# Edge lists of a graph attention layer: third quarter's rest shared by eight lanes, and five pieces of work moved to other steps

## The chip, the cores and the metric

One core of one Trainium2 chip. The metric is the device time of one execution in microseconds (us), median of the runs.

## What is computed

One layer of graph attention, then a second graph layer, over 4096 nodes of 128 features and a 4096 x 4096 matrix `adj`:

```python
h = jnp.maximum(_layernorm(x, axis=-1), 0.0)
Wh = h @ W;  e_src = Wh @ a[:d_out];  e_dst = Wh @ a[d_out:]
e = leaky_relu(e_src[:, None] + e_dst[None, :], 0.2)
mask = (adj > 0) | eye(N);  e = where(mask, e, NEG_INF)
x = x + softmax(e, axis=1) @ Wh
h = jnp.maximum(_layernorm(x, axis=-1), 0.0)
weights = where(adj < 1.0, sens(adj), 0.0)      # sens(0) = 0
x = x + weights @ (h @ W1 + B)
```

`adj` holds zeros and ones and is sparse. Where every entry is at least 1 or has a sensitivity of zero, the second layer adds nothing. So the kernel checks every entry (is it 0 or at least 1?), and only if a check, or one of the bounds on list lengths, fails, does it run a general path. These inputs don't take that path.

## The kernel before

**The stream.** `adj` is 64 MB and is read once, in 32 chunks of 2 MB (128 x 4096 fp32) into a ring of six (`adj_ring`), by SyncE's queue. Four quarters (s = 0 to 3) of 1024 rows each have eight chunks: 16 steps of two chunks. Chunks 24 to 31 are the fourth quarter. A slot of the ring is loaded again when its chunk was packed by TensorE and checked by VectorE (13 chunks, line 1129, one pass) or ScalarE (19 chunks, line 947, two passes).

**Packing and scanning.** TensorE turns eight rows' edges and the column number into one word per column (`pack`, L629 and L642). VectorE takes the eight largest words of every segment (`scan`, L1172), and, at the end of a piece of steps, the largest of these (`pick`, L1191): the edges of a lane of eight rows.

**Own and shared slots.** Five pieces (`PIECES`: steps, slots, own, shared, lanes). The first slots of each lane are its own: groups of 8 gathers. What is beyond them (the rest) is merged over 4 or 8 lanes, as many as the last number says (`place` merges on TensorE, L699; `pick_shared` takes the best 32 on VectorE, L1221 to L1249; `place_shared`, L719; `decode_shared` makes the index, L1278, and the masks). A group of shared slots has 32 / lanes gathers: 8 with four lanes, 4 with eight.

**Groups.** In all ten, g = 0 to 9. Piece 1: groups 0, 1 and shared 2; piece 2: 3, 4 and shared 5; piece 3 (third quarter): own group 6, shared group 7; piece 4 (steps 12 to 14): own group 8, its rest being handed to piece 5 (step 15): shared group 9, gathered one by one. For each, GpSimd issues one indirect DMA per slot (L544, 128 rows of the node table each), in the order of the groups. Group g waits until group g - 4 was scattered. Then `weigh` on VectorE (edge weights L1348, L1351; spreading to lanes, L1359, L1365 or L1372) and `scatter` on TensorE (L769) add them to the quarter's sums in PSUM. `add_columns` (L754) and `add_own` (L761) add two further parts; `epilogue` (VectorE, L1453 and L1458) divides and adds to x; a store follows.

**The order.** Each engine runs a loop over the chunks, i = 0 to 31, with what it does at i from tables by hand (`SCAN_AT`, `WEIGH_AT`, `SCATTER_AT`, `EPILOGUE_AT`, `CHECK_LATE` and so on). In VectorE's loop the order at one i is: early checks, `decode`, `decode_shared`, `column` (L1442), `scan`, `pick`, late checks (`CHECK_LATE`), hub, `weigh`, `epilogue`. At the end of its loop VectorE has `weigh(7)`, `scan(15)`, `pick(4)`, `epilogue(2)`, `pick_shared(4)`, `decode_shared(4)`, `weigh(8)` and then group 9 slot by slot, with the fourth quarter's result in three parts (`weigh_last`, L1387 and L1398; `finish_last`, L1468 and L1472).

Of the kernel before, what the change touches and what calls it, by code (L numbers as in the profile page):

```python
# [74 lines left out]
PIECES = [((0, 1, 2, 3), 32, 16, 32, 4), ((4, 5, 6, 7), 24, 16, 16, 4), ((8, 9, 10, 11), 24, 8, 32, 4),  # L75
# [46 lines left out]
CHECK_LATE = {22: 22, 27: 26, 29: 28}  # L122
# [6 lines left out]
QUAD_SCORES_AT, PAIR_SCORES_AT, OCT_SCORES_AT = 2, 4, 5  # L129
# [7 lines left out]
WEIGH_AT = {13: 0, 17: 1, 18: 2, 21: 3, 25: 4, 26: 5, 28: 6}  # L137
SCATTER_AT = {14: 0, 17: 1, 19: 2, 22: 3, 26: 4, 27: 5, 30: 6}
# [3 lines left out]
ADD_COLUMNS_AT = {13: 0, 21: 1, 28: 2}  # L142
EPILOGUE_AT = {20: 0, 28: 1}
OWN_WEIGHTS_AT = {8: 0, 17: 1, 22: 2, CHUNKS: 3}
ADD_OWN_AT = {13: 0, 21: 1, 29: 2}


def gnn_program(nc, x, adj, w0, a0, w1, b1, out):
# [13 lines left out]
    with ctx:  # L162
# [3 lines left out]
        def sem(name):  # L166
# [73 lines left out]
        r_quad = sb("r_quad", [P, 2, KB * 32])  # L240
# [50 lines left out]
        oct_on = shared_on[:, (len(SHARES) - 1) % 2, :, :, :].rearrange("p e k q -> p (e k q)").rearrange(  # L291
            "p (e k c) -> p e k c", k=KB, c=OL)
# [5 lines left out]
        s_by_oct = general_mem[:, NB * 32:NB * 32 + KB * KB * OL]  # L298
# [252 lines left out]
        def _(pe):  # L551
# [121 lines left out]
            def hub_group(m):  # L673
                pe.wait_ge(hub_w_set, m + 1)
                if m == 0:
                    pe.wait_ge(r_quad_set, 5)
# [44 lines left out]
            def quad_scores(pair):  # L721
                if pair:
                    pe.wait_ge(r_quad_set, 1)
                pe.wait_ge(s_by_quad_set, 1)
                pe.wait_ge(shared_set, 7)
                if pair:
                    nc.tensor.matmul(bank[7][:, 0:KB * 32], same_pair, s_by_quad[:, KB * 32:2 * KB * 32], start=True,
                                     stop=True).then_inc(quads_done, 1)
                else:
                    nc.tensor.matmul(bank[7][:, :], same_quad,  # L730
                                     s_by_quad.rearrange("p (h o n) -> p o h n", h=2, o=2)[:, 0, :, :], start=True,
                                     stop=True).then_inc(quads_done, 1)

            def oct_scores():
                pe.wait_ge(r_quad_set, 3)
                pe.wait_ge(s_by_oct_set, 1)
                pe.wait_ge(oct_set, 4)
                nc.tensor.matmul(bank[7][:, :], same_oct, s_by_oct, start=True, stop=True).then_inc(quads_done, 1)
# [78 lines left out]
            for i in range(CHUNKS):  # L817
                pack(i)
                if chunk(i)[0] == 0 and i % 2 == 0:
                    if i == 0:  # L820
                        pe.wait_ge(r_rows_set, 2)
                    turn_hub(i)
                if chunk(i)[1] == 0:
                    turn_columns(i)
                if i == QUAD_SCORES_AT:
                    quad_scores(0)
                if i == PAIR_SCORES_AT:
                    quad_scores(1)
                if i == OCT_SCORES_AT:
                    oct_scores()  # L830
# [18 lines left out]
            scatter(7)  # L849
# [53 lines left out]
        def _(act):  # L903
# [110 lines left out]
            for i in range(CHUNKS):  # L1014
                for s, half in ROW_WEIGHTS_AT.get(i, ()):
                    row_weights(s, half)
                if i == QUAD_SCORES_AT + 1:
                    act.wait_ge(quads_done, 1)
                    nc.scalar.activation(r_quad[:, :, :].rearrange("p s n -> p (s n)"), bank[7][:, :], ACT.Exp,
                                         scale=-(1 - SLOPE)).then_inc(r_quad_set, 1)  # L1020
                if i == PAIR_SCORES_AT + 1:
                    act.wait_ge(quads_done, 2)
                    for h in range(2):
                        part = slice(h * P // 2, (h + 1) * P // 2)
                        nc.scalar.activation(r_pair[part, :].rearrange("p (u n) -> p u n", u=HK),
                                             bank[7][part, 0:KB * 32].rearrange("p (u h n) -> p h u n", u=HK, h=2)[:, h, :, :],
                                             ACT.Exp, scale=-(1 - SLOPE)).then_inc(r_quad_set, 1)
                if i == OCT_SCORES_AT + 2:
                    act.wait_ge(quads_done, 3)
                    for h in range(2):  # L1030
                        part = slice(h * P // 2, (h + 1) * P // 2)
                        nc.scalar.activation(r_oct[part, :].rearrange("p (u n) -> p u n", u=HK),
                                             bank[7][part, :].rearrange("p (u h n) -> p h u n", u=HK, h=2)[:, h, :, :],
                                             ACT.Exp, scale=-(1 - SLOPE)).then_inc(r_quad_set, 1)
# [5 lines left out]
                if i == CHUNKS - 1:  # L1040
                    own_weights(SG - 1)
# [38 lines left out]
        def _(dve):  # L1080
# [127 lines left out]
            def pick_shared(n):  # L1208
# [4 lines left out]
                merge_to = oct_words[:, LEFT:LEFT + w] if n == HANDED + 1 else shared_cand[0:sets, 0:w]  # L1213
# [38 lines left out]
            def decode_shared(n):  # L1252
# [4 lines left out]
                on = oct_on if lanes == OL else shared_on[:, o % 2, 0:w, :, :]  # L1257
# [67 lines left out]
            def edge_weights(g):  # L1325
# [3 lines left out]
                if g == 0:  # L1329
                    dve.wait_ge(r_slots_set, 1)  # L1330
                    dve.wait_ge(r_quad_set, 5)
                if IS_SHARED[g]:
                    o = SHARES.index(n)
                    dve.wait_ge(shared_on_set, o + 1)
                    per = KB * HK
                    r_of = (r_quad[:, s // 2, :] if w == KB else r_pair[:, :]).rearrange("p (e n) -> p e n", n=per)
                    weight = shared_w[:, 0:w, :, :].rearrange("p e k q -> p e (k q)")
                    on = shared_on[:, o % 2, 0:w, :, :].rearrange("p e k q -> p e (k q)")
# [14 lines left out]
            def spread_weights(g):  # L1353
# [10 lines left out]
                elif w == GE:  # L1364
# [4 lines left out]
                        ALU.mult).then_inc(spread_set, 1)  # L1369
                else:  # L1370
# [9 lines left out]
            def weigh_last(e):  # L1380
# [8 lines left out]
                                               oct_on[:, e, :, :].rearrange("p k c -> p (k c)"), ALU.max,  # L1389
# [147 lines left out]
            for n, (col, op, neg) in enumerate(((DD, ALU.max, False), (DD, ALU.min, True),  # L1537
# [8 lines left out]
            quads = (SG - 1) * KB  # L1546
# [9 lines left out]
            nc.vector.tensor_tensor(s_by_oct.rearrange("p (n x) -> p n x", n=KB),  # L1556
                                    whe[:, quads:NB, SS:SS + 1].broadcast_to([P, KB, KB * OL]),
                                    kc_of_m.rearrange("p (o k) c -> p o (k c)", o=1).broadcast_to([P, KB, KB * OL]),
                                    ALU.mult).then_inc(s_by_oct_set, 1)

            for i in range(2, CHUNKS):
# [42 lines left out]
            pick(4)  # L1604
            epilogue(2)
# [107 lines left out]
```

## Time and profile before

| | us |
|---|---|
| median of 3 runs (lowest, highest) | 216.37 (216.04, 217.75) |
| the profiled execution's time | 217.44 |
| its span | 215.6 |
| VectorE busy | 182.0 (84%) |
| ScalarE busy | 189.3 (88%) |
| TensorE busy | 154.3 (72%) |
| GpSimd busy | 132.8 (62%) |
| chain that ended last: DMA, VectorE, TensorE | 36%, 31%, 18% |
| adjacency loads, 32 | 67 MB of 76.8 MB in all |

All instants below are us from the span's start, of the one profiled execution. The chain of work that ended last has the stream of `adj_ring` until 165.4, and from then on pieces of VectorE and TensorE, with GpSimd's gathers between 202.4 and 208.5. Idle time matters only where that chain runs.

### The profile page before, as it was taken

The page shows a single profiled execution, that of the slowest core. Times are in us where ns is not written, and L with a number is a line of the kernel's source. Part 1 is how long each engine was busy: PE and PEld are TensorE (multiplying, and loading weights), DVE is VectorE, ACT ScalarE, POOL GpSimd, SP SyncE. Part 2 cuts the span into 40 slices and gives each one's busy share as a digit, 9 for nine tenths or more (in the row PEclk, how much of TensorE's full clock was granted, in tenths as well). Part 3 has the DMA queues.
Part 4 walks back from the last instruction along what each step waited for, and adds up shares of the span by engine and source line. Part 5 has one row for each costly group of instructions (what it writes and reads, how often), then busy time and mean ns, then how long its engine had stood idle before and what let it go on. Part 6 is the DMA issues. An engine that isn't in the chain of part 4 may idle for free.

```text
span 215.6 us, 3229 instructions
## 1 busy us (share of the span) xinstructions
PE 154.3 (72%) x956; PEld 103.7 (48%) x970; DVE 182.0 (84%) x535; ACT 189.3 (88%) x207; POOL 132.8 (62%) x140
## 2 busy tenths in 40 slices
PE   0186779983794992989929997499392977799472
PEld 0074565440362760549615844186341654668361
DVE  7993999999979999999488796995986499878855
ACT  0699987599899999999999999799999994999960
POOL 3980002295000588888878888888787788667450
PEclk9999999996599698599985999999979799999995
DMA  5999999999999999999999999999999999961303
GB/s 166 355 413 410 410 408 408 409 411 405 418 418 409 409 393 405 391 400 393 402 388 387 394 401 394 404 387 400 394 387 389 386 401 393 406 229 43 115 23 103
DMA packets 22259, 76.81 MB, mean 356 GB/s; under 512 B 2527, under 2 KB 3126, under 8 KB 22240
## 3 DMA queue, kind: packets, MB, share of 16 engines
q1 hardware_dynamic: 18912, 71.31, 84.7%
q0 software_dynamic: 2912, 5.22, 7.0%
q8 instruction: 8, 0.13, 0.2%
q10 hardware_dynamic: 416, 0.07, 0.2%
q14 instruction: 11, 0.09, 0.1%
HBM read 74.06 MB, written 4.23 MB: 363 GB/s over the span
## 4 chain that ended last, share of the span: by engine, by line
DMA 36%; DVE 31%; PE 18%; issue 7%; ACT 5%; SPq 1%; POOL 1%; POOLq 0%; DVEq 0%
DMA adj_ring<-in_adj 35%; DVE summed L1134 10%; PE bank L642 9%; DVE cand L1172 3%; ACT spread L921 3%; DVE hub_w L1415 3%; PE bank L769 2%; DVE x_sb L1458 2%; PE bank L754 2%; PE bank L761 2%; SPq L383 1%; DMA gathered_rows<-node_table,shared_index 1%; DVE stats L1114 1%; PE bank L629 1%; DVE shared_slots L1230 1%
## 5 line engine op out<-in xcount | busy, mean ns | idle before, releaser
L544 POOL DMA_INDIRECT gathered_rows<-node_table,index x48 | 76.0, 1584 | 36.5 <-DVE index L1309 22.5
L952 ACT ACTIVATE trash_a<-adj_ring,below_one 128x4096 fp8e4<-128x4096 f32 x19 | 70.4, 3705 | 5.7 <-DMA adj_ring<-in_adj 5.2
L642 PE MATMUL bank<-adj_ring,pack_w 128*128 128x512 bf16 (+3 forms) x255 | 70.0, 402 | 2.4 <-DMA adj_ring<-in_adj 1.5
L961 ACT ACTIVATE trash_a<-adj_ring 128x4096 fp8e4<-128x4096 f32 x19 | 68.7, 3614 | 0.5
L1134 DVE SCALAR_TENSOR_TENSOR summed<-adj_ring 128x4096 fp8e4<-128x4096 f32 x13 | 58.0, 4458 | 4.3 <-DMA adj_ring<-in_adj 4.2
L642 PEld LDWEIGHTS bank<-adj_ring,pack_w 128*128 128x128 bf16 x262 | 26.1, 104 | 31.5 <-issue 8.8
L544 POOL DMA_INDIRECT gathered_rows<-node_table,shared_index x24 | 33.2, 1382 | 9.6 <-issue 6.7
L1172 DVE MAX8 cand<-bank 128x8 f32<-128x120 f32 (+25 forms) x82 | 23.3, 351 | 3.9 <-PE bank L642 3.9
L769 PE MATMUL bank<-gathered_rows,spread 128*128 128x129 f32 x160 | 20.9, 282 | 3.9 <-DVE spread L1398 2.4
L769 PEld LDWEIGHTS bank<-gathered_rows,spread 128*128 128x128 f32 x160 | 19.4, 194 | 5.1 <-issue 4.8
L629 PE MATMUL bank<-codes,code_w 128*128 128x512 bf16 x25 | 11.2, 448 | 8.5 <-DMA adj_ring<-in_adj 5.6
L678 PE MATMUL bank<-whe,hub_w 128*128 128x129 f32 x64 | 10.4, 316 | 5.1 <-DVE hub_w L1419 5.0
L921 ACT ACTIVATE spread<-x_sb,shift,rstd 128x128 f32<-128x128 f32 x32 | 13.2, 497 | 0.3 <-DVE shift L1126 0.3
L678 PEld LDWEIGHTS bank<-whe,hub_w 128*128 128x128 f32 x64 | 9.1, 219 | 7.0 <-DVE hub_w L1419 6.8
L491 POOL PARTITION_ALL_REDUCE ends_all<-ends x1 | 1.4, 1442 | 17.3 <-DVE ends L1539 17.3
L565 PE MATMUL bank<-ident,spread 128*128 128x128 f32 x32 | 6.3, 327 | 7.8 <-ACT spread L921 7.8
L577 PE MATMUL bank<-w_sb,gathered_rows 128*128 128x130 f32 x64 | 9.8, 300 | 1.4 <-ACT whe L935 1.3
L1442 DVE SCALAR_TENSOR_TENSOR col_w<-r_rows,hub_whe,bank 128x512 f32<-128x512 f32 (+1 forms) x6 | 4.2, 708 | 7.4 <-PE bank L609 7.4
L629 PEld LDWEIGHTS bank<-codes,code_w 128*128 128x128 bf16 x32 | 3.7, 115 | 13.7 <-DMA adj_ring<-in_adj 6.2
L577 PEld LDWEIGHTS bank<-w_sb,gathered_rows 128*128 128x128 f32 x64 | 8.6, 208 | 2.7 <-ACT gathered_rows L927 2.4
L985 ACT ACTIVATE own_w<-ident,w_self 128x128 f32<-128x128 f32 x32 | 9.7, 386 | 0.0
L699 PE MATMUL bank<-slots,own_lane 128*32 128x16 f32 (+1 forms) x24 | 1.4, 188 | 10.5 <-issue 10.5
(190 smaller groups left out, 258.4 us busy)
## 6 DMA issues: line engine op xcount, KB each, us to landing
adj_ring<-in_adj SPq DMA_DIRECT2D x32, 2048.0 KB, 23.6
node_table<-gathered_rows POOLq DMA_DIRECT2D x4, 520.0 KB, 8.3
x_sb<-in_x SPq DMA_DIRECT2D x8, 256.0 KB, 5.9
out<-x_sb SPq DMA_DIRECT2D x3, 512.0 KB, 14.2
gathered_rows<-node_table,index POOLq DMA_INDIRECT x48, 5.9
gathered_rows<-node_table,shared_index POOLq DMA_INDIRECT x24, 5.4
out<-x_sb SPq DMA_DIRECT2D x2, 192.0 KB, 2.1
out<-x_sb SPq DMA_DIRECT2D x1, 128.0 KB, 1.9
```

What stands on the lines that cost most here:

```text
L544: pool.indirect_dma_start(out=rows[:, g % RING_GROUPS * GE + t, :], out_offset=None, in_=table, in_offset=bass.IndirectOffsetOnAxis(ap=row ...
L577: last = nc.tensor.matmul(bank[6 + half][:, b * (D + 2):(b + 1) * (D + 2)], hT[:, nb * P:(nb + 1) * P], w0_sb[:, :], start=(b == 0), stop= ...
L629: nc.tensor.matmul(to[:, :], code_w[:, 2 * c + half, :], codes[:, :], start=True, stop=False, skip_group_check=True)
L642: last = nc.tensor.matmul(to[:, lo:hi], pack_w[:, k, :], ring_hi[:, i % AR, row_at + lo:row_at + hi], start=False, stop=(k == KB - 1), ski ...
L678: last = nc.tensor.matmul(bank[7][:, 0:E1], hub_w[:, m % 2, b, :], whe[:, 4 * HUB_ORDER[m] + b, ONE:ONE + E1], start=(m + b == 0), stop=(m ...
L769: return nc.tensor.matmul(acc_of(SUPER_OF_GROUP[g], t), spread[:, g % 2, at * KB:(at + 1) * KB, :], rows[:, g % RING_GROUPS * GE + turn, G ...
L921: last = nc.scalar.activation(hn_block(b), x_sb[:, b, :], ACT.Identity, bias=shift[:, b:b + 1], scale=rstd[:, b:b + 1])
L952: nc.scalar.activation(trash_a[:, :], ring[:, i % AR, :], ACT.Sign, bias=below_one[:, :], scale=-1.0, accum_out=signs[:, n:n + 1], saturat ...
L961: nc.scalar.activation(trash_a[:, :], ring[:, i % AR, :], ACT.Abs, accum_out=sizes[:, n:n + 1], saturate=False).then_inc(checked_a, 1)
L985: last = nc.scalar.activation(own_w[:, t, :], ident[:, :], ACT.Copy, scale=w_self[:, nb:nb + 1])
L1134: nc.vector.scalar_tensor_tensor(trash_v, ring[:, i % AR, :], 1.0, ring[:, i % AR, :], ALU.is_ge, ALU.not_equal, accum_out=bad_v[:, n:n + ...
L1172: last = nc.vector.max(cand[:, at * 8:(at + 1) * 8], word_bank(step, half)[:, lo:hi])
```

## The change

- Piece 3 merges its rest over eight lanes (`PIECES`, last number 4 to 8). Group 7 then has 4 gathers, not 8; `place(2)` merges eight pieces, not four; `pick_shared(2)` works on 16 x 128 words. Its table of scores is an "oct" one: two of these are made now (`s_by_oct`, `r_oct2`), and the quad and pair scores take one half of a bank each, at one step.
- VectorE checks chunk 26 at step 26 (was 27), chunk 28 at 28 (was 29). In one step the order becomes hub, `epilogue`, `weigh`, late check.
- `weigh(6)` at 27 (was 28), `weigh(7)` at 28 (was behind the loop); `scatter(4)`, `(5)`, `(6)`, `(7)` at 25, 26, 28, 29 (were 26, 27, 30, behind the loop).
- `add_columns(2)`, `add_own(2)` and `epilogue(1)` at 27 (were 28, 29, 28).
- `epilogue(2)` at 31, ahead of `scan(15)` (was behind `pick(4)`).
- `own_weights(3)` on ScalarE at 29, ahead of the check of chunk 29 (was ahead of that of chunk 31).

```diff
-((4, 5, 6, 7), 24, 16, 16, 4), ((8, 9, 10, 11), 24, 8, 32, 4),
+((4, 5, 6, 7), 24, 16, 16, 4), ((8, 9, 10, 11), 24, 8, 32, 8),
-CHECK_LATE = {22: 22, 27: 26, 29: 28}
+CHECK_LATE = {22: 22, 26: 26, 28: 28}
-QUAD_SCORES_AT, PAIR_SCORES_AT, OCT_SCORES_AT = 2, 4, 5
+QUAD_SCORES_AT, OCT_SCORES_AT = 2, (4, 5)
-WEIGH_AT = {13: 0, 17: 1, 18: 2, 21: 3, 25: 4, 26: 5, 28: 6}
-SCATTER_AT = {14: 0, 17: 1, 19: 2, 22: 3, 26: 4, 27: 5, 30: 6}
+WEIGH_AT = {13: 0, 17: 1, 18: 2, 21: 3, 25: 4, 26: 5, 27: 6, 28: 7}
+SCATTER_AT = {14: 0, 17: 1, 19: 2, 22: 3, 25: 4, 26: 5, 28: 6, 29: 7}
-ADD_COLUMNS_AT = {13: 0, 21: 1, 28: 2}
-EPILOGUE_AT = {20: 0, 28: 1}
-OWN_WEIGHTS_AT = {8: 0, 17: 1, 22: 2, CHUNKS: 3}
-ADD_OWN_AT = {13: 0, 21: 1, 29: 2}
+ADD_COLUMNS_AT = {13: 0, 21: 1, 27: 2}
+EPILOGUE_AT = {20: 0, 27: 1, 31: 2}
+OWN_WEIGHTS_AT = {8: 0, 17: 1, 22: 2, 29: 3}
+ADD_OWN_AT = {13: 0, 21: 1, 27: 2}
...
+                elif SET_LANES[PIECE_OF_GROUP[g]] == OL:
+                    for x in range(2):
+                        last = nc.vector.tensor_tensor(
+                            spread[:, g % 2, x * w * KB:(x + 1) * w * KB, :].rearrange("p e (o c) -> p e o c", o=2),
+                            oct_w[:, 0:w, :, :].rearrange("p e k (o c) -> p (e k) o c", o=1).broadcast_to(
+                                [P, w * KB, 2, OL]),
+                            quad_of_e[:, 2 * x:2 * x + 2].rearrange("p (o q c) -> p o q c", o=1, c=1).broadcast_to(
+                                [P, w * KB, 2, OL]), ALU.mult)
+                    last.then_inc(spread_set, 1)
...
             dve.wait_ge(oct_set, 2)
-            nc.vector.tensor_tensor(s_by_oct.rearrange("p (n x) -> p n x", n=KB),
...
+            for n in range(2):
+                blocks = slice((2 + n) * KB, (3 + n) * KB)
+                nc.vector.tensor_tensor(s_by_oct[n].rearrange("p (n x) -> p n x", n=KB),
...
+                for m in HUB_AT.get(i, ()):
+                    hub(m)
+                if i in EPILOGUE_AT:
+                    epilogue(EPILOGUE_AT[i])
+                if i in WEIGH_AT:
+                    weigh(WEIGH_AT[i])
                 if i in CHECK_LATE:
                     check(CHECK_LATE[i])
-                for m in HUB_AT.get(i, ()):
-                    hub(m)
-                if i in WEIGH_AT:
-                    weigh(WEIGH_AT[i])
-                if i in EPILOGUE_AT:
-                    epilogue(EPILOGUE_AT[i])
-            weigh(7)
             scan(STEPS - 1)
             pick(4)
-            epilogue(2)
             pick_shared(4)
```

## Rows read from the trace of the kernel before

**Rows 1.** Page, the span in 40 slices of 5.39 us: busy share of the DMA engines

```profile
DMA  5999999999999999999999999999999999961303
```

**Rows 2.** The 32 adjacency loads: from issue to landing

```profile
DMA to landing us min/median/max: 11.1/23.6/27.2
```

**Rows 3.** VectorE's timeline: start, us, line, operation, idle time before and its releaser

```profile
164.76 0.73 DVE L1372 TENSOR_TENSOR spread<-same,hq_of_e 128x512 f32<-128x512 f32 x1
169.84 0.75 DVE L1442 SCALAR_TENSOR_TENSOR col_w<-r_rows,hub_whe,bank 128x512 f32<-128x512 f32 x1 [4.35 <-PE bank L609]
170.51 4.42 DVE L1134 SCALAR_TENSOR_TENSOR summed<-adj_ring 128x4096 fp8e4<-128x4096 f32 x1
...
176.78 0.20 DVE L1348 TENSOR_TENSOR edge_w<-r_slots,gathered_rows 128x64 f32<-128x64 f32 x1
...
177.28 1.22 DVE L1359 TENSOR_TENSOR spread<-edge_w,lane_of_p 128x1024 f32<-128x1024 f32 x1
...
180.70 4.42 DVE L1134 SCALAR_TENSOR_TENSOR summed<-adj_ring 128x4096 fp8e4<-128x4096 f32 x1
...
188.86 0.17 DVE L1309 SCALAR_TENSOR_TENSOR index<-words_i,empty_i 128x8 int32<-128x8 int32 x1
...
190.98 0.43 DVE L1348 TENSOR_TENSOR same<-r_quad,gathered_rows 128x256 f32<-128x256 f32 x1 [0.41 <-DMA gathered_rows<-node_table,shared_index]
...
194.59 1.43 DVE L1172 MAX8 cand<-bank 128x8 f32<-128x272 f32 x4 [1.47 <-PE bank L642]
...
196.69 2.16 DVE L1458 SCALAR_TENSOR_TENSOR x_sb<-bank,rden,x_sb 128x128 f32<-128x128 f32 x8
...
202.19 0.16 DVE L1278 TENSOR_TENSOR shared_index<-shared_column,shared_empty 128x4 int32<-128x4 int32 x1
```

**Rows 4.** GpSimd's timeline in the same form: gathers of groups 6 to 9

```profile
166.08 1.00 POOL L544 DMA_INDIRECT gathered_rows<-node_table,index  x1 [0.30 <-issue]
...
171.29 4.50 POOL L544 DMA_INDIRECT gathered_rows<-node_table,shared_index  x1 [0.30 <-issue]
...
177.41 1.97 POOL L544 DMA_INDIRECT gathered_rows<-node_table,shared_index  x1 [0.30 <-issue]
...
180.98 5.01 POOL L544 DMA_INDIRECT gathered_rows<-node_table,shared_index  x1 [0.30 <-issue]
...
189.80 1.08 POOL L544 DMA_INDIRECT gathered_rows<-node_table,index  x1 [2.77 <-DVE index L1309]
...
203.13 1.01 POOL L544 DMA_INDIRECT gathered_rows<-node_table,shared_index  x1 [2.60 <-DVE shared_index L1278]
```

**Rows 5.** TensorE's timeline, same form: chunks 26 and 28 packed, place(4)

```profile
165.46 0.39 PE L629 MATMUL bank<-codes,code_w 128*128 128x512 bf16 x1 [4.03 <-DMA adj_ring<-in_adj]
...
167.49 1.91 PE L642 MATMUL bank<-adj_ring,pack_w 128*128 128x512 bf16 x4
...
177.00 0.39 PE L629 MATMUL bank<-codes,code_w 128*128 128x512 bf16 x1 [1.35 <-DMA adj_ring<-in_adj]
177.23 1.07 PE L642 MATMUL bank<-adj_ring,pack_w 128*128 128x512 bf16 x4
...
196.42 0.54 PE L699 MATMUL bank<-slots,own_oct 128*16 128x8 f32 x16
```

**Rows 6.** From issue to landing, gathers of group 7: at 169.99, then at 180.98

```profile
DMA to landing us min/median/max: 5.4/5.4/5.4
...
DMA to landing us min/median/max: 9.9/9.9/9.9
```

**Rows 7.** One stretch: busy us of PE, PEld, DVE, ACT, POOL; granted clock, DMA, GB/s

```profile
166.00:169.40 3.40, 3.40 (x11) 1.23 (x10) 0.00 (x0) 3.37 (x3) 2.71 (x3) 0.51 1.03 392
```

**Rows 8.** Timeline: table of oct scores on VectorE, its exponentials on ScalarE

```profile
34.56 0.68 DVE L1556 TENSOR_TENSOR spread<-whe,bits_i 128x512 f32<-128x512 f32 x1
...
60.47 0.77 ACT L1032 ACTIVATE r_oct<-bank 64x256 f32<-64x256 f32 x2
```

**Rows 9.** ScalarE's timeline: the first pass of its check of chunk 29

```profile
182.26 3.71 ACT L952 ACTIVATE trash_a<-adj_ring,below_one 128x4096 fp8e4<-128x4096 f32 x1 [3.13 <-DMA adj_ring<-in_adj]
```

More of the change, by code:

```diff
@@ L290, in gnn_program @@
         oct_w = shared_mem.rearrange("p (e k c) -> p e k c", k=KB, c=OL)
-        oct_on = shared_on[:, (len(SHARES) - 1) % 2, :, :, :].rearrange("p e k q -> p (e k q)").rearrange(
-            "p (e k c) -> p e k c", k=KB, c=OL)
+        oct_on = [shared_on[:, o % 2, :, :, :].rearrange("p e k q -> p (e k q)").rearrange(
+            "p (e k c) -> p e k c", k=KB, c=OL) for o in range(len(SHARES))]
         s_by_quad = general_mem[:, 0:NB * 32]
@@ L297, in gnn_program @@
         oct_words = placed[0:LANES, 1, :]
-        s_by_oct = general_mem[:, NB * 32:NB * 32 + KB * KB * OL]
+        s_by_oct = [general_mem[:, NB * 32 + n * KB * KB * OL:NB * 32 + (n + 1) * KB * KB * OL] for n in range(2)]
         verdict = cand[:, 0:NBAD]
@@ L719, in place_shared, with quad_scores, oct_scores @@
                 nc.tensor.matmul(to[:, SHARED_COL:SHARED_COL + TURNS[n]], words, turns, start=True, stop=True, skip_group_check=True).then_inc(shared_done, 1)
-            def quad_scores(pair):
-                if pair:
-                    pe.wait_ge(r_quad_set, 1)
+            def quad_scores():
                 pe.wait_ge(s_by_quad_set, 1)
                 pe.wait_ge(shared_set, 7)
[L726 to L736, printed above, removed]
+                nc.tensor.matmul(bank[7][:, 0:KB * 32], same_quad, s_by_quad[:, 0:KB * 32], start=True,
+                                 stop=True, skip_group_check=True)
+                nc.tensor.matmul(bank[7][:, KB * 32:2 * KB * 32], same_pair, s_by_quad[:, KB * 32:2 * KB * 32], start=True,
+                                 stop=True, skip_group_check=True).then_inc(quads_done, 1)
+            def oct_scores(n):
+                pe.wait_ge(r_quad_set, 3 + 2 * n)
+                pe.wait_ge(s_by_oct_set, n + 1)
                 pe.wait_ge(oct_set, 4)
-                nc.tensor.matmul(bank[7][:, :], same_oct, s_by_oct, start=True, stop=True).then_inc(quads_done, 1)
+                nc.tensor.matmul(bank[7][:, :], same_oct, s_by_oct[n], start=True, stop=True).then_inc(quads_done, 1)
             def add_columns(s):
@@ L825, in _ @@
                 if i == QUAD_SCORES_AT:
[L826 to L830, printed above, removed]
+                    quad_scores()
+                if i in OCT_SCORES_AT:
+                    oct_scores(OCT_SCORES_AT.index(i))
                 if i in PLACE_AT:
@@ L848, in _ @@
                     place(PLACE_BEHIND[i])
-            scatter(7)
             place(4)
@@ L1212, in pick_shared @@
                 source = bank[4] if n == 0 else bank[7]
-                merge_to = oct_words[:, LEFT:LEFT + w] if n == HANDED + 1 else shared_cand[0:sets, 0:w]
+                if n == HANDED + 1:
+                    merge_to = oct_words[:, LEFT:LEFT + w]
+                elif w > 64:
+                    merge_to = oct_words[:, 0:w]
+                else:
+                    merge_to = shared_cand[0:sets, 0:w]
                 words = oct_words[:, 0:LEFT + w] if n == HANDED + 1 else merge_to
@@ L1334, in edge_weights @@
                     dve.wait_ge(shared_on_set, o + 1)
[L1335 to L1338, printed above, removed]
+                    if SET_LANES[n] == OL:
+                        per = KB * OL
+                        r_of = r_oct2[:, :].rearrange("p (e n) -> p e n", n=per)
+                        weight = oct_w[:, 0:w, :, :].rearrange("p e k c -> p e (k c)")
+                        on = oct_on[o][:, 0:w, :, :].rearrange("p e k c -> p e (k c)")
+                    else:
+                        per = KB * HK
+                        r_of = (r_quad[:, :] if w == KB else r_pair[:, :]).rearrange("p (e n) -> p e n", n=per)
+                        weight = shared_w[:, 0:w, :, :].rearrange("p e k q -> p e (k q)")
+                        on = shared_on[:, o % 2, 0:w, :, :].rearrange("p e k q -> p e (k q)")
                 else:
@@ L1545, in _ @@
             dve.wait_ge(shared_set, 7)
-            quads = (SG - 1) * KB
+            quads = 2 * KB
             nc.vector.tensor_tensor(s_by_quad.rearrange("p (n x) -> p n x", x=32)[:, 0:quads, :],
```

35 lines of the change are left out of this document (17 added, 18 removed).

## The prediction

> **What bounds the kernel now.** Read the page's slices first [rows 1]: the 16 DMA engines are full from the second slice to the 35th, up to about 189 us. That is the stream of 32 chunks, and its loads wait 11.1 us at the least between issue and landing [rows 2], so a further load is always queued and a small delay of an engine early on does not starve it. The change can only matter in the last fifth. Then read VectorE's timeline there [rows 3]. VectorE waits for chunk 26 (4.35 us idle), checks it at 170.51, checks chunk 28 from 180.70 to 185.12, and from then on nearly everything hangs on it: the third gather list (index, 188.86), the last scan (194.59, after 1.47 us idle for TensorE), the third epilogue (to 198.85), the last picks and the last list (shared_index, 202.19). Then read GpSimd's [rows 4]: gathers follow each other every 1.30 us (1.00 and 0.30 of issue). Group 8 starts 0.94 us after its index (189.80), and its eight fill GpSimd to 200.53 (the idle of 2.60 before the next); group 9, the last four, starts at 203.13, again 0.94 us after its index. From there to the span's end it is 12.5 us, of which the change alters almost nothing. So **the gain is the number of us by which group 9 starts sooner.**
>
> **The work that hangs on the check of chunk 28.** Call the end of that check E; now E = 185.12. Group 8's first gather starts at E + 4.7. Group 9's starts at E + 18.0.
>
> **The third epilogue goes ahead of the last scan.** It is 2.16 us of updates, and some 0.2 of reciprocals ahead of them. Now it stands between pick(4) and pick_shared(4). It ends at 198.85, while what pick_shared(4) needs, the merge of place(4) on TensorE, is ready at 196.96 [rows 5]; with about 0.1 us for the hand-over this link shortens by 1.7 us. Scan to index(4) takes 7.6 us now (194.59 to 202.19) and would take 5.9. Part of the epilogue moves into the 1.47 us of idle before the scan. weigh(7) (2.14 us, from 190.98 to the 193.12 at which that idle begins) is moved ahead of the check too. So VectorE's chain from E is: the stretch to index(3), 3.7 us; the rest of its decoding and pick_shared(3), to E + 5.45 (190.57 now); epilogue E + 7.8; index(4) E + 13.7; GpSimd could start at E + 14.6. But GpSimd itself is busy with group 8: E + 4.7 + 8 x 1.30 = E + 15.1. That is the later one. Against E + 18.0 that is **2.9 us gained, less whatever E moves.** This cap on the gain is the first point to see: over 2.9 us needs an earlier E.
>
> **Where E goes.** Now check(28) waits for VectorE, not for data: pack(28) already starts at 177.0 [rows 5]. Its new place is at step 28, but behind weigh(7) in program order, and weigh(7) waits until the last gather of group 7 has landed. So the four gathers must be followed.
> - check(26) starts when weigh(5) ends, 165.49 [rows 3]; the chunk is there at 165.46 [rows 5]. It fills idle time and ends at 169.99. The idle it fills is real, 4.35 us, so on VectorE it costs nothing.
> - On GpSimd it does cost. A gather that meets a check is held until the check is over and then takes 0.87 us: the one at 171.29 took 4.50 us, the one at 180.98 took 5.01, each ending 0.86 us after the check [rows 3, 4]. Sooner, the check meets the eighth gather of group 6 (166.08) instead, which ends at 170.85, and only then do group 7's follow: 171.15, 172.45, 173.75, 175.05. Now group 7's fourth is the one at 171.29, and it ends at 175.79. So the fourth gather ends at about 176.05 in the changed kernel, no sooner than before: halving the group gains four gathers behind that point, not ahead of it.
> - In the stream a gather lands 5.4 us after its issue (the one at 169.99) [rows 6]; a held one landed 4.9 us after its end (180.98 + 9.9 = 190.9, where weigh(7) now waits 0.41 us). Group 6's last lands at about 175.3, so weigh(6), moved one step up, waits for it; VectorE has column(26) and epilogue(1) (2.4 us) to do before, done by about 174. Then weigh(6) (1.7 us, 176.78 to 178.50 now) to 177.0, column(27) (0.7 us, as at 169.84) and scan(13) (1.3 to 1.4 us, less the overlap at its ends) to about 178.9.
> - Group 7's fourth lands at 175.05 + 5.4 = 180.4. weigh(7) takes 2.2 us: to 182.6. check(28): **E = 187.1, 2.0 us later than now.** Queued behind it are scan(14), pick(3) and through them place(3), pack(30) and pack(31) on TensorE and group 8 on GpSimd.
>
> 2.9 - 2.0 = 0.9 us.
>
> A page speaks on the held gathers. The Trainium skill (SBUF — State Buffer, Who interferes with whom) says that a DVE instruction with two SBUF inputs contends with a GpSimd instruction that reads SBUF, but infers that it does not stop descriptor generation. By the inference the sum would have no held gathers; the 4.50 and 5.01 us of this trace are against it for the check.
>
> **TensorE's clock.** TensorE loses scatter(7) and add_own work from its end and takes it earlier: scatter(7) runs at 184.1 to 186.1 and then the engine waits in order for pick(3), about 3.6 us. Before chunk 26 it was idle for 4.03 us [rows 5] and the stretch after that was granted 0.51, the 1.2 GHz level; four matmuls that take 1.07 us at full clock took 1.91 there [rows 5, 7]. If this repeats, pack(30) takes up to 1.7 us more and pack(31) ends near 195.8, while VectorE is free for the scan at E + 7.8 = 194.9. Then index(4) comes at 195.9 + 5.9 = 201.8 and group 9 at 202.7: 0.4 us gained. I find the low level likelier than not, and the bounds are 0.4 and 0.9: I take 0.6.
>
> **Small things.** One more product of scores on VectorE ahead of the loop, 128x512, 0.68 us less about 0.3 for the shorter one of quads; two more exponentials on ScalarE, 0.77 us together in the like case [rows 8]. Both are covered by the queued stream; uncovered they would cost 0.4 and 0.8. pick_shared(2) works on 16x128 in place of 32x64: four rounds at some 0.1 us more each, hidden behind the wait for chunk 25. ScalarE has 3.13 us idle before it checks chunk 29, where the last own_weights (2.43 us) fits [rows 9]; this frees its end, which sets nothing. The clean-up of edges and the store at the end keep their length.
>
> **Sum.** The profiled execution has a span of 215.6 and a time of 217.44; the median shown is 216.37, 1.1 below it. The gain goes to the median: 216.37 - 0.6 = **215.8**.
>
> **Rivals.**
> - *Check(28) comes in time.* It needs group 7 by 178.9. If gathers were not held by the check, group 6 would end at 167.08 and group 7's fourth at 172.3, landed by 177; weigh(7) would then run 178.9 to 181.1, E = 185.5, and group 9 would gain 2.5 us: 213.9. With VectorE finding chunk 28 a little sooner still, E = 185.1 and 2.9 us: 213.5. For it: the chunk is there at 177.0, and 5.4 us from issue to landing is long and may scatter. Against it: two held gathers out of two checks in the stretch. 0.22. (The inference of the page named above would make this the outcome.)
> - *Group 7's last gather is held again, now by weigh(6).* The gather at 177.41 took 1.97 us, until 0.88 us after the spread of 177.28 [rows 3, 4]. weigh(6)'s spread now begins at about 175.8; the gather begins at 175.05. It slips past by 0.7 us. If it begins behind that point, it ends at 177.8 and lands at 182.2: E = 188.9, 3.8 us late, and 0.9 us are lost, with the clock 1.4: 217.3 to 217.8. It is slower than before, though inside 1%. 0.15.
> - *Between the two*, with E about 1 us late: 1.3 to 2.2 us gained, 214.2 to 215.1. 0.10.
> - *The early work is not covered* or the order on TensorE stalls the stream (place(3) now holds pack(30)): over 2.2 us lost. The stream ends at 189 to 192 whatever they do. 0.04.
> - The forecast itself, 0 to 1.3 us gained (215.1 to 216.4): 0.49.
>
> **How the numbers follow.** A change under 1% (2.2 us) is about what a measurement of this kernel cannot tell from none. Faster by over 1% means below 214.2, which only the first rival gives: 0.22. Slower by over 1%: 0.04. Within: 0.74. The likeliest case's own range is 215.1 to 216.4. For 8 in 10 it must take in most of the first rival (from 213.7) and most of the second (to 217.2).
>
> **What would show it.** In the changed trace: a check by VectorE from 165.5 and a gather of some 4.7 us that ends near 170.9; VectorE idle before weigh(7) for the landing of a shared gather, around 179 to 180.4; the check of chunk 28 starting at 182.6, not 180.7; the first own gather of group 8 at 191.8; group 9 starting at the end of group 8 with only issue between; the 0.5 level granted somewhere in 190 to 194. I am wrong if check(28) starts before 181.5 (then near 213.8), or if the gather around 175 takes over 2 us (then over 217).

## The result

| | us |
|---|---|
| before, median of 20 runs (lowest, highest) | 216.56 (215.85, 217.90) |
| changed, median of 20 runs (lowest, highest) | 218.45 (216.53, 220.82) |
| ratio, with its 95% interval | 1.0073 (1.0053 to 1.0094) |
| changed, the profiled execution: time, span | 219.13, 217.3 |

The changed kernel is slower by 0.7% (1.6 us by the ratio, 1.9 by the medians), where 0.6 us less was forecast; 218.45 lies above the range of 213.7 to 217.2. Every ratio in this document is to runs of the kernel before taken beside it, and leaves out runs over 1.5% above the fastest of the same kernel, which the medians keep. The chain that was followed in the prediction is the one that runs, but two of its terms were sized too small and one that was taken as fixed was not. The runs also spread over 4.3 us, where those of before spread over 2.1. All instants are of one profiled execution of each kernel.

VectorE's timeline of the changed kernel, to be held against [rows 3]:

```profile
166.15 4.41 DVE L1125 SCALAR_TENSOR_TENSOR summed<-adj_ring 128x4096 fp8e4<-128x4096 f32 x1
...
175.90 0.23 DVE L1350 TENSOR_TENSOR edge_w<-r_slots,gathered_rows 128x64 f32<-128x64 f32 x1 [2.38 <-issue]
...
181.21 0.43 DVE L1350 TENSOR_TENSOR same<-r_oct,gathered_rows 128x256 f32<-128x256 f32 x1 [1.63 <-issue]
...
183.34 4.42 DVE L1125 SCALAR_TENSOR_TENSOR summed<-adj_ring 128x4096 fp8e4<-128x4096 f32 x1
...
191.73 0.17 DVE L1305 SCALAR_TENSOR_TENSOR index<-words_i,empty_i 128x8 int32<-128x8 int32 x1
...
197.50 1.43 DVE L1163 MAX8 cand<-bank 128x8 f32<-128x272 f32 x4 [1.74 <-PE bank L643]
...
203.34 0.17 DVE L1274 TENSOR_TENSOR shared_index<-shared_column,shared_empty 128x4 int32<-128x4 int32 x1
```

The check of chunk 26 has moved into VectorE's idle time (166.15, was 170.51). weigh(6) then idles 2.38 us, weigh(7) 1.63 us, both for gathers. The check of chunk 28 starts at 183.34, not at 180.70, and ends at E = 187.76 (E is the end of that check, as in the prediction), 2.6 us later than before. The last scan starts 2.9 us later; the last list comes only 1.15 us later, since the epilogue is no longer behind the scan.

GpSimd's timeline, against [rows 4], and the landing of the last gather of group 7 (that at 175.64):

```profile
166.81 4.62 POOL L545 DMA_INDIRECT gathered_rows<-node_table,index  x1 [0.30 <-issue]
...
175.64 1.00 POOL L545 DMA_INDIRECT gathered_rows<-node_table,shared_index  x1 [0.30 <-issue]
...
192.68 1.08 POOL L545 DMA_INDIRECT gathered_rows<-node_table,index  x1 [12.77 <-DVE index L1305]
...
204.28 0.99 POOL L545 DMA_INDIRECT gathered_rows<-node_table,shared_index  x1 [1.38 <-DVE shared_index L1274]
205.57 1.60 POOL L545 DMA_INDIRECT gathered_rows<-node_table,shared_index  x1 [0.30 <-issue]
```

```profile
DMA to landing us min/median/max: 5.5/5.5/5.5
```

The check holds the eighth gather of group 6 for 4.62 us; it ends 0.87 us after the check. 175.64 + 5.5 = 181.1 is when weigh(7) can start. GpSimd, which issued gathers until 186 before, is now idle for 12.77 us before group 8: it has four gathers fewer, and nothing uses the time.

TensorE's timeline, and its stretches in the columns of [rows 7]:

```profile
184.08 1.95 PE L765 MATMUL bank<-gathered_rows,spread 128*128 128x129 f32 x16
190.32 0.57 PE L700 MATMUL bank<-slots,own_oct 128*16 128x8 f32 x16 [4.29 <-issue]
...
191.65 1.91 PE L643 MATMUL bank<-adj_ring,pack_w 128*128 128x512 bf16 x4 [0.23 <-issue]
...
193.78 3.68 PE L643 MATMUL bank<-adj_ring,pack_w 128*128 128x512 bf16 x12
```

```profile
186.50:189.90 3.40, 0.00 (x0) 0.00 (x0) 3.33 (x11) 3.40 (x2) 0.00 (x0) 0.82 1.00 407
189.90:193.30 3.40, 2.75 (x22) 1.65 (x24) 2.34 (x14) 3.37 (x3) 0.62 (x1) 0.50 0.43 174
193.30:196.70 3.40, 3.40 (x12) 1.28 (x11) 2.45 (x12) 3.37 (x4) 2.49 (x4) 0.68 0.19 46
```

After scatter(7) TensorE stands idle for 4.29 us, since the next in its order is place(3), which waits for pick(3). The granted clock falls to 0.50, the 1.2 GHz level, at about 188.7, while it is idle, and stays there until about 195.5: for place(3), pack(30) and most of pack(31). That is what the last scan waits for (1.74 us idle).

### The profile page after: what moved, and what is told of

Its sections match the earlier page's. It is cut to its first block, busy times and chain, and to the rows that moved or that the text cites. A ratio compares the mean times of both kernels' runs of the same rounds, so it can differ in the third digit from the quotient of the medians.

```text
span 217.3 us, 3245 instructions
## 1 busy us (share of the span) xinstructions
PE 155.6 (72%) x966; PEld 106.0 (49%) x980; DVE 183.2 (84%) x537; ACT 190.0 (87%) x209; POOL 122.7 (56%) x136
## 4 chain that ended last, share of the span: by engine, by line
DMA 36%; DVE 23%; PE 21%; issue 10%; ACT 7%; SPq 1%; POOL 1%; POOLq 0%; DVEq 0%; ACTq 0%
DMA adj_ring<-in_adj 35%; PE bank L643 10%; DVE summed L1125 8%; ACT spread L914 3%; DVE hub_w L1426 3%; PE bank L765 2%; ACT trash_a L945 2%; PE bank L750 2%; PE bank L757 2%; DVE cand L1163 1%; DMA gathered_rows<-node_table,shared_index 1%; DVE stats L1105 1%; PE bank L700 1%; SPq L384 1%; PE bank L630 1%
## 5 line engine op out<-in xcount | busy, mean ns | idle before, releaser
L545 POOL DMA_INDIRECT gathered_rows<-node_table,index x48 | 78.5, 1635 | 48.0 <-DVE index L1305 34.3
L545 POOL DMA_INDIRECT gathered_rows<-node_table,shared_index x20 | 20.5, 1027 | 7.2 <-issue 5.8
L630 PE MATMUL bank<-codes,code_w 128*128 128x512 bf16 x24 | 10.4, 435 | 5.5 <-DMA adj_ring<-in_adj 3.0
L578 PE MATMUL bank<-w_sb,gathered_rows 128*128 128x130 f32 x64 | 10.6, 318 | 1.2 <-ACT whe L928 0.9
L578 PEld LDWEIGHTS bank<-w_sb,gathered_rows 128*128 128x128 f32 x64 | 9.5, 227 | 2.4 <-ACT gathered_rows L920 2.1
L1426 DVE TENSOR_SCALAR hub_w<-r_hub,whe 128x128 f32<-128x128 f32 x32 | 8.8, 351 | 0.0
L566 PEld LDWEIGHTS bank<-ident,spread 128*128 128x128 f32 x32 | 4.5, 173 | 8.4 <-ACT spread L914 7.3
```

Of the source, the lines that this page charges most:

```text
L545: pool.indirect_dma_start(out=rows[:, g % RING_GROUPS * GE + t, :], out_offset=None, in_=table, in_offset=bass.IndirectOffsetOnAxis(ap=row ...
L578: last = nc.tensor.matmul(bank[6 + half][:, b * (D + 2):(b + 1) * (D + 2)], hT[:, nb * P:(nb + 1) * P], w0_sb[:, :], start=(b == 0), stop= ...
L630: nc.tensor.matmul(to[:, :], code_w[:, 2 * c + half, :], codes[:, :], start=True, stop=False, skip_group_check=True)
L1426: last = nc.vector.tensor_scalar(hub_w[:, m % 2, b, :], r_hub[:, :], whe[:, nb, QA:QA + 1], whe[:, nb, AA:AA + 1], ALU.mult, ALU.max)
```

## The experiments

Theory A is the prediction's chain with the measured sizes: check(26) holds a gather, group 7 lands late, weigh(7) waits for it ahead of check(28), E is late, and the hole this leaves at TensorE brings the low clock. Rival B: only the clock costs, wherever the check stands. Rival C: the epilogue ahead of the last scan delays the scan by what it saves. Rival D: fewer gathers pay by themselves.

**1. Check first, then weigh(7).** The table of VectorE's steps has weigh(7) one step later.

```diff
-WEIGH_AT = {..., 27: 6, 28: 7}
+WEIGH_AT = {..., 27: 6, 29: 7}
```

> The changed kernel with weigh(7) one step later, at 29, so that VectorE checks chunk 28 before it waits for group 7's last gather. Theory A (the end E of check(28) is late because of that wait, and with it index(3), pack(30) and the clock): check(28) starts at about 179.6 and ends at 184.1 in place of 187.8; weigh(7) runs 184.1 to 186.3; scan(14) starts at 186.3, 1.5 us sooner than in the changed kernel; TensorE's long idle (186.0 to 190.3) is cut in two by scatter(7), so pack(30) and pack(31) run at full clock; scan(15) at 194.2 instead of 197.5; time about 215.0, that is 1.5 us under the kernel before and 3.3 under the changed one. Rival B (the order of check and weigh is nothing, what costs is the low clock at TensorE that comes of the moved scatters): no faster than the changed kernel, 218. Rival C (the epilogue ahead of the last scan costs as much as it gives): at most the 1.5 us of E come back, 217.

Measured: 216.11 us, ratio to before 0.9974 (0.9943 to 1.0005). Its VectorE timeline:

```profile
178.63 4.40 DVE L1125 SCALAR_TENSOR_TENSOR summed<-adj_ring 128x4096 fp8e4<-128x4096 f32 x1
182.96 0.42 DVE L1350 TENSOR_TENSOR same<-r_oct,gathered_rows 128x256 f32<-128x256 f32 x1
185.08 1.48 DVE L1163 MAX8 cand<-bank 128x8 f32<-128x24 f32 x5
...
188.89 0.17 DVE L1305 SCALAR_TENSOR_TENSOR index<-words_i,empty_i 128x8 int32<-128x8 int32 x1
...
194.20 1.43 DVE L1163 MAX8 cand<-bank 128x8 f32<-128x272 f32 x4 [1.28 <-PE bank L643]
...
200.94 0.16 DVE L1274 TENSOR_TENSOR shared_index<-shared_column,shared_empty 128x4 int32<-128x4 int32 x1
```

Theory A holds: one entry of a table takes the wait off the path, the last scan comes at 194.20 as said, and 2.3 us of the changed kernel's time come back (216.11 against 218.45; the two intervals are apart). Rivals B and C allowed 218 and 217. But 1.1 us of the expected gain are missing. Of these the profile shows 0.9: from scan(15) to index(4) it is 6.74 us, not 5.9. TensorE's timeline shows why, and its stretch:

```profile
196.49 3.70 PE L750 MATMUL bank<-hub_whe,col_w 128*128 128x129 f32 x16
200.12 0.38 PE L720 MATMUL bank<-turn_of_tq,stats 16*128 16x4 f32 x2
```

```profile
196.70:200.00 3.30, 3.30 (x16) 3.20 (x15) 2.26 (x13) 3.27 (x4) 2.69 (x3) 0.50 0.21 47
```

add_columns(3) met a stretch at the low clock (granted 0.50 from 196.7 to 200.0; 3.70 us, not 2.05) and place_shared(4) stands behind it.

**2. Keep TensorE busy.** 15 matmuls into a bank nobody reads, between scatter(7) and place(3):

```diff
                 if i in SCATTER_AT:
                     scatter(SCATTER_AT[i])
+                if i == 29:
+                    filler(15)        # waits for scan(13), then bank[2] <- code_w, codes
```

> The changed kernel with 15 matmuls of 128x512 (3.3 us of TensorE at full clock) into a bank that nobody reads, between scatter(7) and place(3), where TensorE was idle for 4.29 us. Their result is thrown away. Theory A's clock term: the granted clock stays at 1.00 through pack(30) and pack(31), which then end near 195.5 in place of 197.5; scan(15) starts at about 195.8 when the third epilogue is over, group 9 starts at 202.9 (bounded by group 8 on GpSimd) instead of 204.3; time 1.4 us under the changed kernel, about 217.1, still not below the kernel before. Rival: the low clock is hidden and E alone decides: 218.4, as the changed kernel.

Measured: 217.84 us, ratio 1.0045 (1.0018 to 1.0073). The granted clock is 1.00 in all three stretches above. One of them, then VectorE, GpSimd and TensorE:

```profile
189.90:193.30 3.40, 3.17 (x29) 1.78 (x30) 2.61 (x18) 3.40 (x2) 1.04 (x1) 1.00 0.49 199
```

```profile
195.25 1.41 DVE L1171 MAX8 cand<-bank 128x8 f32<-128x272 f32 x4
...
204.20 0.23 DVE L1358 TENSOR_TENSOR edge_w<-r_slots,gathered_rows 128x64 f32<-128x64 f32 x1 [2.06 <-DMA gathered_rows<-node_table,index]
```

```profile
202.77 1.00 POOL L545 DMA_INDIRECT gathered_rows<-node_table,shared_index  x1 [0.30 <-issue]
```

```profile
206.09 5.00 PE L765 MATMUL bank<-gathered_rows,spread 128*128 128x129 f32 x28 [3.46 <-DVE spread L1369]
```

On the chain the clock term is real, in its place and size: the scan starts 2.25 us sooner (195.25) with E nearly the same (187.6), and group 9 starts at 202.77, 1.5 us sooner, directly behind group 8. The median falls by only 0.6 us (217.1 was expected), and its interval overlaps the changed kernel's, so what the clock costs in time is not shown. The profile shows where the rest is lost: weigh(8) now waits 2.06 us for group 8's last gather, and TensorE's next sums fall into a low stretch (5.00 us for 28 matmuls from 206.09; in the changed kernel 20 took 2.47). So the end of the kernel is not a constant behind group 9. From group 9's first gather to the span's end it is 12.5 us before, 13.0 changed, 13.8 here.

**3. No held gather.** Chunk 26 isn't checked at all.

```diff
-DVE_CHECKED = [..., 22, 26, 28]
+DVE_CHECKED = [..., 22, 28]      # and 26 not in ACT_CHECKED either
```

> The changed kernel without the check of chunk 26 (that part of the computation is left out: entries of chunk 26 are not checked). Theory A: the gather of group 6 at 166.8 is not held, takes 1.00 us, and the four gathers of group 7 are issued at 168.1 to 172.0 instead of 171.7 to 175.6 and land by 177.5; weigh(6) starts at 173.7, weigh(7) at about 177.6, check(28) at 179.8 and ends at 184.2, 3.5 us sooner than in the changed kernel; time about 214.5. Rival (landing time in the stream, not the held gather, sets weigh(7)): check(28) starts within 1 us of where it does now (183.3), time over 217.5.

Measured: 215.68 us, ratio 0.9957 (0.9931 to 0.9983); 214.5 was expected. GpSimd, VectorE, then TensorE:

```profile
167.04 1.00 POOL L545 DMA_INDIRECT gathered_rows<-node_table,index  x1 [0.30 <-issue]
```

```profile
177.88 0.43 DVE L1350 TENSOR_TENSOR same<-r_oct,gathered_rows 128x256 f32<-128x256 f32 x1 [1.46 <-issue]
180.02 4.44 DVE L1125 SCALAR_TENSOR_TENSOR summed<-adj_ring 128x4096 fp8e4<-128x4096 f32 x1
```

```profile
191.64 1.98 PE L643 MATMUL bank<-adj_ring,pack_w 128*128 128x512 bf16 x8 [1.51 <-DMA adj_ring<-in_adj]
```

The same gather takes 1.00 us, not 4.62; weigh(7) and check(28) come 3.3 us sooner. The held gather is the cause of the late landing: from issue to landing group 7's last gather takes 5.6 us here, 5.5 in the changed kernel. VectorE has 4.4 us less to do here as well, but it idles 1.46 us for the gathers before weigh(7), so its own work is not what sets the start. The earlier E also takes the low clock off pack(30) and pack(31) (1.00 from 186 to 196), so this run doesn't price the two apart. The last scan starts 3.8 us sooner (193.66) and group 9 3.4 us (200.84); the median falls by 2.8. With E at 184.5 chunk 31 has become the bound: pack(31) at 191.64 waits for it, so an E earlier still would not bring the last scan sooner.

**4. The epilogue back behind pick(4).**

```diff
-EPILOGUE_AT = {20: 0, 27: 1, 31: 2}
+EPILOGUE_AT = {20: 0, 27: 1}
             pick(4)
+            epilogue(2)
             pick_shared(4)
```

> The changed kernel with the third epilogue back behind pick(4), where the kernel before had it. The claim of the prediction is that this link alone is worth 1.7 us between scan(15) and index(4). Theory A: scan(15) still starts at 197.5 (TensorE decides it), index(4) comes at 205.1, not 203.3; time 1.7 us over the changed kernel, about 220.1. Rival C (the epilogue delays the scan by about what it saves): same time as the changed kernel, 218.4.

Measured: 219.60 us (four runs), ratio 1.0101 (1.0040 to 1.0162). VectorE:

```profile
198.21 1.43 DVE L1163 MAX8 cand<-bank 128x8 f32<-128x272 f32 x4 [4.62 <-PE bank L643]
...
205.81 0.16 DVE L1274 TENSOR_TENSOR shared_index<-shared_column,shared_empty 128x4 int32<-128x4 int32 x1
```

The last list comes 7.60 us behind the scan; in the changed kernel it is 5.84. So the link is worth 1.76 us in the profiles, and the last scan does not start sooner for the epilogue's absence, which is against rival C. In time it is not shown: the median is 1.15 us over the changed kernel's, but both spread by more than that and the intervals overlap.

**5. Each half of the change alone.** Lanes: `PIECES` and the tables of scores as changed, all steps as before. Moves: the steps as changed, `PIECES` as before.

```diff
-((8, 9, 10, 11), 24, 8, 32, 4),      lanes_only has the 8, moves_only the 4
+((8, 9, 10, 11), 24, 8, 32, 8),
```

> Only the lanes of the third piece go from four to eight (four gathers, not eight, and the tables of scores that this needs); every check, weigh, scatter, epilogue and own_weights stays at the step of the kernel before. Theory A: the fifth to eighth gather of group 7 stood behind the point that matters nowhere on the path (in the kernel before check(28) does not wait for them and weigh(7) waited only 0.41 us), so check(28) ends at 185.1 to 185.5 and index(3) comes at about 189 as before; time the same as before within 0.3 us, 216.4 to 216.8. Rival D (fewer gathers free the stream and GpSimd, and that alone pays): at least 1 us under the kernel before, 215.5.

> Only the moves, with four lanes and eight gathers in group 7 as before. Theory A: weigh(7), now ahead of check(28), waits for the eighth gather, issued at about 181 and landed at 186.5; weigh(7) to 188.7, check(28) ends at E = 193, 5.3 us later than in the changed kernel; scan(15) near 202, group 9 at 209; time 5 us over the changed kernel, about 223. Rival B (what costs is only the clock at TensorE, not the wait for the gathers): about the changed kernel's 218.4.

Measured: lanes alone 217.07 us, ratio 0.9997 (0.9969 to 1.0025); moves alone 225.42 us, ratio 1.0380 (1.0340 to 1.0419). Halving group 7 is worth nothing that can be measured by itself, against rival D, and seven us once the moves are there (218.45 against 225.42). The moves alone cost 8.6 us against the kernel before, more than the 6.5 expected: E is 193.6 (193 was said), and then the granted clock is 0.50 again, from about 195.6 to 202.5; TensorE was idle for 3.37 us between scatter(7) and place(3). VectorE, moves alone:

```profile
189.17 4.42 DVE L1131 SCALAR_TENSOR_TENSOR summed<-adj_ring 128x4096 fp8e4<-128x4096 f32 x1
...
203.88 1.42 DVE L1169 MAX8 cand<-bank 128x8 f32<-128x272 f32 x4 [2.29 <-PE bank L642]
```

**6. Towards a better version.** All four have weigh(7) at 29 and place_shared(4) ahead of add_columns(3). `shared_first` has only this; `shared_first_filled` adds seven filler matmuls ahead of place(4); `fill_two` adds eight more ahead of scatter(7); `fill_three` five more ahead of pack(31).

```diff
             place(4)
-            add_columns(SG - 1)
             place_shared(4)
+            add_columns(SG - 1)
```

> The changed kernel with weigh(7) at 29, and on TensorE place_shared(4) ahead of add_columns(3). In the run with weigh(7) at 29 alone, add_columns(3) fell into a stretch at the low clock, took 3.70 us and ended only at 200.1, while shared_slots were ready at about 199.0. If that is what took the last 0.9 us, index(4) comes 5.9 us after scan(15), at 200.1 and not 200.9, group 9 starts at 201.0, and the time is 0.8 us under that run: 215.3, clearly under the kernel before. Rival: GpSimd's eight gathers of group 8 or the add_columns and add_own behind it (4 us, up to 7 at the low clock) become the bound and hold scatter(8): no gain over that run, 216.1.

> As shared_first, with seven more matmuls of 128x512 whose result nobody reads (1.5 us at full clock) between pack(31) and place(4), where TensorE idles 1.9 us. If the low clock after pack(31) is what makes add_columns(3) and add_own(3) long, the granted clock stays at 1.00 to 204 and the time is equal to shared_first or up to 0.5 us under it: 214.8 to 215.3. Rival: the filler, at 3 us if it falls into the low clock itself, holds up place(4): slower than shared_first by up to 1 us.

> As shared_first_filled, with eight further matmuls of 128x512, result unread, between pack(29) and scatter(7), where TensorE idles 1.2 to 2.8 us. In the profile of shared_first a stretch at the low clock fell on scatter(7) (3.63 us and not 2.02) and made index(3) 1.5 us later than in shared_first_filled; that it falls there in some executions and not in others would be why these kernels spread over 3 us while the kernel before spreads over 2. Expected: granted clock 1.00 from 178 on in every profile, index(3) at 189, index(4) at 200, group 9 at 200.5 to 201; time 215.0, at least 1.2 us under the kernel before, and a spread no wider than before's. Rival (the clock was not what spread them): 216.2, as shared_first_filled.

> As fill_two, with five more such matmuls between pack(30) and pack(31), where TensorE waits 1.3 us for chunk 31. Expected: equal to fill_two within 0.3 us (215.0), since pack(31) already runs at full clock there; up to 0.5 us faster if the low stretch at 199.3 to 202.7 that shared_first_filled still had goes away with it.

| | median | ratio to before |
|---|---|---|
| shared_first | 216.50 | 0.9991 (0.9971 to 1.0011) |
| shared_first_filled | 216.19 | 0.9978 (0.9951 to 1.0004) |
| fill_two | 215.50 | 0.9942 (0.9915 to 0.9968) |
| fill_three | 215.76 | 0.9950 (0.9923 to 0.9977) |

From shared_first, TensorE:

```profile
186.30 3.63 PE L765 MATMUL bank<-gathered_rows,spread 128*128 128x129 f32 x16 [2.84 <-DVE spread L1374]
```

The link did shorten as expected (5.96 us from scan to index in shared_first), but it gave nothing over experiment 1, and 215.3 was missed: in that profile scatter(7) took 3.63 us at the low clock, place(3) came late and so did index(3), at 191.06.

In the profile of fill_two scatter(7) takes 2.02 us and index(3) comes at 189.45. But shared_first_filled, without the filler ahead of scatter(7), has 2.02 us and 189.56 as well. fill_two's median is 0.7 us lower and its interval clearly below before, yet it overlaps that of shared_first_filled, so what this filler is worth stays open.

The spread of fill_two is 2.4 us (2.7 in shared_first_filled, 1.8 in the runs of before beside fill_two), so it is hardly narrower, and the profile of fill_two still has a low stretch at add_columns(3), which takes 3.81 us: "1.00 from 178 on" and a spread no wider than before's were wrong. fill_three is equal to fill_two within 0.3 us, as said, but not at the 215.0 that was said for both.

**7. The last slot first.** In fill_two the fourth slot was weighed at 209.93, behind finish_last(0), which idled for TensorE.

```diff
             weigh_last(2)
-            finish_last(0)
             weigh_last(3)
+            finish_last(0)
```

> As fill_two, and on VectorE the fourth slot of group 9 is weighed before the first part of the fourth quarter is finished (weigh_last(3) ahead of finish_last(0)). In fill_two the fourth gather had landed at 207.3, but its weighing started at 209.93, behind finish_last(0), which had waited 1.59 us for TensorE. Expected: weigh_last(3) at 207.4, the last matmul near 209.5 instead of 211.5; time 1 to 1.5 us under fill_two, 214.2. Rival (finish_last's three parts on VectorE, not the fourth slot, end the kernel): the same as fill_two, 215.5.

> As swap_last, with nine unread matmuls of 128x512 between place(4) and place_shared(4), where TensorE idles 2.66 us, and six between add_own(3) and scatter(8), so that no long idle stands ahead of scatter(8). In fill_two add_columns(3) and add_own(3) ran at the low clock (3.81 and 3.05 us, not 2.05 each) and held scatter(8) to 206.05. Expected: granted clock 1.00 to 210, scatter(8) at 205, time 0.5 us under swap_last, 213.7. Rival (the matmuls themselves delay place_shared or scatter(8) where they fall into a low stretch): equal or up to 0.5 us over swap_last.

Measured: swap_last 215.14 us (six runs), ratio 0.9907 (0.9870 to 0.9944); swap_last_filled 215.75 us, ratio 0.9948 (0.9923 to 0.9974). VectorE in swap_last:

```profile
208.34 0.28 DVE L1407 SCALAR_TENSOR_TENSOR same<-r_oct,gathered_rows,shared_on 128x64 f32<-128x64 f32 x1 [0.56 <-DMA gathered_rows<-node_table,shared_index]
208.66 0.49 DVE L1418 TENSOR_TENSOR spread<-same,quad_of_e 128x128 f32<-128x128 f32 x2
209.07 0.17 DVE L1488 RECIPROCAL rden<-bank 128x3 f32<-128x3 f32 x1
```

The slot is weighed 1.6 us sooner. Of this the profiles' spans show less (214.8 and 214.2): beside weigh(8)'s spread the third gather took 2.03 us here, and 1.00 in fill_two. The expected 214.2 was missed. The intervals of fill_two and swap_last overlap, so the swap's own price stays open; against before, swap_last is 0.9% faster, with the lowest median of all (six runs). The last fillers did hold the clock at 1.00 from 186 to 211, but 213.7 was expected and the median is 0.6 us above swap_last's, with overlapping intervals: the full clock there gave nothing that can be measured, as the rival allowed.

## Where the prediction was right and wrong

The steps that failed are terms of the sum: the low clock at TensorE was taken too short (at most 0.5 us of group 9's start, measured 1.5), and the end of the kernel behind group 9 was taken as fixed (it grew by 0.5 us, and by 1.3 where the clock was held). E was 0.7 us late on top.

- **What is on the path: right.** Held gather, wait at weigh(7), late check, and all that hangs on it came in the order given. Experiments 1 and 3 each take one link away, and the check of chunk 28 starts within 1 us of what was expected of them. E does not give its gain one for one: in experiment 1 it is 4.7 us sooner and group 9 only 2.4. One sign did not come: group 9 was to follow group 8 on GpSimd with only issue between, and GpSimd stood idle for 1.38 us before it, waiting for the last list.
- **TensorE's clock: right mechanism, the mis-sized term.** "pack(31) ends near 195.8" came out as 197.5. I took the length of the low stretch from one row, 3.4 us [rows 7]; this one held from about 188.7 to 195.5, 5.2 us of it with TensorE at work on place(3) and both chunks. The term was put at up to 0.5 us of group 9's start; experiment 2 shows 1.5. In the time of the kernel that run gives back 0.6 us, which is not clear of noise.
- **"The change alters almost nothing" behind group 9: wrong, a term put at nothing.** From group 9's first gather to the span's end it is 12.5 us before and 13.0 changed. Of this some 0.3 us come up to VectorE's last instruction: beside weigh(8)'s spread at 205.08 the second gather of group 9 took 1.60 us (205.57), where it took 1.22 before. What the rest is isn't shown. Experiments 2 and 6 show up to 13.8 us where group 9 follows group 8 at once. So the cap of 2.9 us could not have been reached as stated either.
- **E: 187.1 forecast, 187.8 measured.** The list of words of the third quarter came 0.8 us later than before (155.90, was 155.11), 0.5 of it there at the scan ahead of it already (150.94, was 150.45). pick_shared(2) was priced rightly (2.9 us for 2.4), and its 0.5 us did fit the wait for chunk 25, of 0.48 us; but then no wait was left to take up the late list, check(26) started 0.66 us later, and all behind it moved along. Whether the list is late for the change stays open: in the other runs of the same steps that scan starts between 149.8 and 151.4 and check(26) between 165.0 and 166.3.
- **The moved epilogue: right.** 5.84 us from scan to list against 5.9; experiment 4 has 1.76 for 1.7.
- **Sum.** Group 9 was to start between 202.2 and 202.7 and started at 204.28: 0.7 from E, and 0.9 to 1.4 from the clock. Then 0.5 us more at the end. The profiled span went from 215.6 to 217.3.
- **The rivals.** "Held again by weigh(6)" has the time that comes nearest (217.3 to 217.8, with the clock) but not the cause: the gather at 175.64 took 1.00 us. "Check(28) comes in time" fell for the reason given. Neither of the two signs of being wrong came (check(28) before 181.5, the gather near 175 over 2 us), and the time was above the range all the same: its upper end had every rival with a low stretch of the one length, and with nothing lost behind group 9.
- **How small a change can be told.** Under 1% was said to be about what can't be told from none. With 20 runs of each kernel the interval was 0.4% wide, and a loss of 0.7% is clear of it.
- **Not tried.** No run takes back the moves of scatter(4) to (6), add_columns(2), add_own(2), epilogue(1) or own_weights(3) one by one; what each is worth is only argued.

## What to carry to other kernels

Moving a check into idle time of its own engine is free only if no other engine's issue is held by it; follow the issues, and the waits that stand behind their landings. Before a wait is put ahead of a long instruction, ask what the instruction needed: here the check needed nothing of what was waited for, and one step later in the table was worth 2.3 us. Work moved off an engine leaves a hole. At TensorE such a hole (4.29 us here, 4.03 before) came with half the clock for the work behind it, and how long that lasted differed from case to case: don't take its length from one row.

## What the runs showed of the hardware that was not expected

- The low clock with an idle stretch of 4.03 us lasted 3.4 us (from 166.0, before), with one of 4.29 us about 6.8 us (from 188.7, changed), of which the first 1.6 us were still idle. 15 matmuls in the hole kept the clock at 1.00. Shorter holes near the end were followed by a low stretch as well (experiment 1: idle for 1.34 and 1.86 us, then 0.50 from 196.7 to 200.0), but not always: the hole of 1.86 us before 199.32 in the changed kernel was not.
- Not gathers alone are held by the check. In the run with weigh(7) at 29, GpSimd's small tensor_scalar of 128x16 that takes 0.29 us in the changed kernel took 4.39 us from 178.78, under the check at 178.63 to 183.03:

```profile
178.78 4.39 POOL L525 TENSOR_SCALAR sd_sum<-shift 128x16 f32<-128x16 f32 x1 [2.99 <-ACT trash_a L954]
```

- The Trainium skill (SBUF — State Buffer, Who interferes with whom) has that contention for a GpSimd instruction that reads SBUF beside a DVE instruction with two SBUF inputs; the trace agrees. It also infers that a tensor_tensor does not hold up descriptor generation. The gathers, which GpSimd issues, took 1.97, 1.60 and 2.03 us beside weigh's spread, a tensor_tensor (before, changed, swap_last), and 4.62 us beside the check, against 1.00 us in experiment 3; the measurement decides that they are held. Whether it is the making of descriptors that waits or the reading of the index, no run here separates.
- A gather landed 5.5 us after its issue under the full stream (the one at 175.64, changed) and 2.4 us after it once the stream was over: the one at 203.13 before, weighed at 205.59.
